# A Mamba-2 mixer's decays: repeated rows loaded from memory and subtracted on ScalarE, in place of a product on TensorE

## The reference

```
proj = hidden @ in_proj_w.T                    # gate, (x, B, C), dt
xBC  = silu(causal_conv4(proj[x, B, C]))       # 4 taps per channel
dt_p = softplus(dt + dt_bias);  A = -exp(A_log)
for t:  state = state * exp(dt_p*A)[t] + (dt_p*x)[t] * B[t]     # 64 heads, 64 x 128
        y[t]  = state @ C[t]
y    = y + x*D;  yn = group_rms(y) * norm_weight * silu(gate);  out = yn @ out_proj_w.T
```

## Time and profile before

| what | value |
|---|---|
| time, median of 3 runs | 1298.97 us |
| the profiled execution | 1300.67 us |
| its span in the trace | 1298.9 us |
| TensorE busy | 1230.5 us, 95% |
| VectorE busy | 933.9 us, 72% |
| ScalarE busy | 702.5 us, 54% |
| GpSimd busy | 653.6 us, 50% |
| moved by DMA | 57.52 MB, 44 GB/s |

### The profile page before, as it was taken

The page is one execution under the profiler, slowest core; times in us unless marked ns, Lnnn a source line. Parts: engine busy times, 40 slices in busy tenths (PEclk is TensorE's granted clock), DMA queues, the critical chain, the costliest instruction groups (busy, mean ns, idle before and its releaser), DMA issues. The chain is left out here.

```text
span 1298.9 us, 22009 instructions
## 1 busy us (share of the span) xinstructions
PE 1230.5 (95%) x6680; PEld 968.9 (75%) x6690; DVE 933.9 (72%) x1735; ACT 702.5 (54%) x1056; POOL 653.6 (50%) x707
## 2 busy tenths in 40 slices
PE   5999999999999999999999999999679999889976
PEld 4777777787778778777778878777557777667754
DVE  5786778669667866966886696688567555479995
ACT  3676676567567666756766675665543333222210
POOL 5057546655655655565465556545653343433330
PEclk9999999999999999999999999999789999889996
DMA  5111021011102101110210110010103322211100
GB/s 178 46 50 34 2 67 34 19 34 49 33 1 66 33 17 33 50 32 1 66 32 17 33 58 24 5 34 2 41 17 115 97 90 83 93 49 48 45 16 25
DMA packets 44233, 57.52 MB, mean 44 GB/s; under 512 B 10117, under 2 KB 21159, under 8 KB 43929
## 3 DMA queue, kind: packets, MB, share of 16 engines
q1 hardware_dynamic: 44185, 56.92, 14.3%
HBM read 49.95 MB, written 6.96 MB: 44 GB/s over the span
## 5 line engine op out<-in xcount | busy, mean ns | idle before, releaser
L722 DVE SCALAR_TENSOR_TENSOR conv<-p_tile,conv_taps,conv 128x511 f32<-128x511 f32 x189 | 141.3, 748 | 51.4 <-ACT conv L583 36.4
L831 DVE TENSOR_TENSOR em<-em,p_gb 128x512 f32<-128x512 f32 x128 | 82.1, 683 | 69.6 <-ACT em L630 69.5
L527 POOL TENSOR_TENSOR squares<-squares 128x256 f32<-128x256 f32 x64 | 48.0, 750 | 132.5 <-ACT squares L656 132.5
L94 PE MATMUL p_tile<-xn_hi,wc_hi 128*128 128x512 f32 x252 | 110.8, 440 | 0.9 <-DVE halo L726 0.9
L656 ACT ACTIVATE squares<-y 128x512 f32<-128x512 f32 x64 | 40.4, 631 | 112.5 <-DVE y L867 111.5
L722 DVE SCALAR_TENSOR_TENSOR conv<-p_gate,conv_taps,conv 128x511 f32<-128x511 f32 (+2 forms) x90 | 67.0, 745 | 46.7 <-ACT conv L583 43.1
L94 PE MATMUL p_tile<-xn_lo,wc_hi 128*128 128x512 f32 x252 | 98.8, 392 | 0.0
L94 PE MATMUL p_d<-wr_hi,zt_hi 128*128 128x512 f32 x236 | 94.0, 398 | 1.5 <-ACT em L630 1.5
L94 PE MATMUL p_d<-wr_lo,zt_hi 128*128 128x512 f32 x236 | 93.1, 394 | 0.0
L495 POOL TENSOR_TENSOR x_w<-xs,head_g 128x512 f32<-128x512 f32 x56 | 58.4, 1043 | 68.7 <-ACT xs L624 63.6
L588 ACT ACTIVATE xbc<-conv 128x512 f32<-128x512 f32 x96 | 60.7, 632 | 59.7 <-DVE conv L730 37.4
(11 more groups left out here) (393 smaller groups left out, 3605.1 us busy)
## 6 DMA issues: line engine op xcount, KB each, us to landing
w_raw<-w SPq DMA_DIRECT2D x108, 256.0 KB, 2.7
q_words<-q SPq DMA_DIRECT2D x33, 256.0 KB, 2.7
h_ring<-h_lo_rows SPq DMA_DIRECT2D x6, 704.0 KB, 4.8
h_lo_rows<-h_rest SPq DMA_DIRECT2D x11, 256.0 KB, 2.1
x_res<-x SPq DMA_DIRECT2D x8, 256.0 KB, 4.1
out<-out_t SPq DMA_DIRECT2D x8, 256.0 KB, 2.0
h_lo_rows<-h_rest SPq DMA_DIRECT2D x11, 128.0 KB, 1.9
gate_second<-w SPq DMA_DIRECT2D x4, 256.0 KB, 5.0
```

The lines of the kernel that those rows point to most:

```text
L94: pe.matmul(out, lhs(k)[0], rhs(k)[n], start=(start and k == 0 and n == 0), stop=False)
L722: ve.scalar_tensor_tensor(out=conv[:, s, sh:], in0=p[:, 0:HALF - sh], scalar=conv_w[:, bass.ds(g, 1), j, tap], in1=conv[:, s, sh:], op0=AL ...
L831: ve.tensor_tensor(m, m, gm.unsqueeze(1).broadcast_to([P, HG // 2, P]), ALU.mult)\
```

## The change

- TensorE's four spreading products (L1085) and two difference products (L1095) go, with their operands and the banks they wrote; `p_d0` and `p_d1` stay as banks of other products.
- cum itself (float32) is written to memory in the prologue, and so is exp(cum), which ScalarE makes there. For each chunk SyncE loads the row of the 8 heads (1024 numbers) into all 128 partitions of `em` (512 KB), and the exp(cum) rows into `e_cum` by two transfers of 64 partitions each, whose pieces are 512 bytes long.
- cum is transposed into a new table `cum_tok` (token on the partition). For the next chunk, ScalarE computes, in place and for each of the 8 heads, max(cum[s] - cum[t], 0) on 128 x 128 elements (`decay_steps`), right behind `z_round`; where the gate tile's SiLU stands behind `z_round`, it now stands behind these eight. In the chunk itself two exponentials with scale -1, in place, complete the decays. No large negative number is needed.
- ScalarE's exponential into `e_cum` goes (L628, L632).
- VectorE's splitting of cum (L961 to L967) goes, a copy into `cum_tok` comes. The transposes of the whole chunk's decay stand behind convolution tile 2 of the prologue, in bank `p_y`, and ScalarE's exponential of them waits there.
- Waits on the two difference banks go (for the output product, the sum of squares, p_in and row transposes); others take their place.

```diff
-        def load_d(g, c):
-            wait(sp, s_d, n - 1)
...
+        def load_cum(g, c):
+
+            n = g * NC + c
+            wait(sp, s_intra, n - 1)
+            row = at(sp, g + c * G)
+            sp.dma_start(em[:, c % 2, :], cum_rows.rearrange("c (g h) t -> (c g) (h t)", g=G)[bass.ds(row, 1), :]
+                         .broadcast_to([P, HG * P])).then_inc(s_dl[c % 2], 16)
+
+        def load_e_cum(g, c):
+
+            wait(sp, s_t, g * (NC - 1) + c - 1)
+            row = at(sp, g + c * G)
+            own = e_rows.rearrange("c (g j a) t -> (c g) a j t", g=G, a=2)[bass.ds(row, 1)]
+            for a in range(2):
+                sp.dma_start(by_tile(e_cum[a * HD:(a + 1) * HD, :]),
+                             own[:, a, :, :].broadcast_to([HD, GW // P, P])).then_inc(s_ecl, 16)
...
             for c in range(NC):
+                if c + 1 < NC:
+                    load_e_cum(g, c + 1)
                 if c + 2 < NC:
-                    load_d(g, c + 2)
+                    load_cum(g, c + 2)
...
+        def decay_steps(g, c):
+
+            act.wait_ge(s_dl[c % 2], 16 * (g * (NC // 2) + c // 2 + 1))
+            for h in range(HG):
+                steps = em[:, c % 2, h * P:(h + 1) * P]
+                made = act.activation(steps, steps, ACT.Relu, scale=-1.0, bias=cum_tok[:, c, bass.ds(g * HG + h, 1)])
+            made.then_inc(s_e, 1)
...
-                act.wait_ge(s_d, n + 1)
-                wait(act, s_intra, n - 1)
-                if last and c >= CH:
-                    act.activation(e_cum[:], p_in[:], ACT.Exp).then_inc(s_ec, 1)
-                for k, p in enumerate((p_d0, p_d1)):
-                    act.activation(em[:, c % 2, k * 512:(k + 1) * 512], p[:], ACT.Exp).then_inc(s_e, 1)
-                if c > 0 and not (last and c >= CH):
-                    act.activation(e_cum[:], p_in[:], ACT.Exp).then_inc(s_ec, 1)
+                act.wait_ge(s_e, 3 * n + 1)
+                for k in range(2):
+                    decay = em[:, c % 2, k * 512:(k + 1) * 512]
+                    act.activation(decay, decay, ACT.Exp, scale=-1.0).then_inc(s_e, 1)
...
                 z_round(n, y_bank(last, c))
+                if c < NC - 1:
+                    decay_steps(g, c + 1)
+                elif not last:
+                    decay_steps(g + 1, 0)
                 if made and c % CH >= 2:
                     gate_silu(CH + n, made[1], made[2], gate_bank(c))
...
+        act.wait_ge(dt_tp, 4)
+        act.activation(by_half(etot_t), transposed(p_y), ACT.Exp).then_inc(dt_ac, 1)
...
-                pe.wait_ge(s_dl[c % 2], 32 * (g * (NC // 2) + c // 2 + 1))
-                if c > 0:
-                    wait(pe, s_t, g * (NC - 1) + c - 1)
-                    for j in range(GW // P):
-                        pe.matmul(p_in[:, j * P:(j + 1) * P], head_rows[:, j, :], d_lhs[:, c % 2, :],
-                                  start=True, stop=True)
-                wait(pe, s_e, 2 * n)
...
-                for k, p in enumerate((p_d0, p_d1)):
-                    mm = pe.matmul(p[:], d_lhs[:, c % 2, :], d_rhs[:, c % 2, k * 512:(k + 1) * 512],
-                                   start=True, stop=True)
-                mm.then_inc(s_d, 1)
...
                 if c > 0:
 
                     pe.wait_ge(s_stu, g * (NC - 1) + c)
-                    pe.wait_ge(s_ec, g * (NC - 1) + c)
+                    wait(pe, s_t, g * (NC - 1) + c - 1)
...
             conv_tile(j, 0, j, 0, (p_tile, p_d1)[j % 2])
+            if j == 2:
+                pe.wait_ge(dt_ve, 12)
+                for b in range(CH):
+                    mm = pe.transpose(p_y[:, b * P:(b + 1) * P],
+                                      t_cum[:, (b + 1) * P - 1:(b + 1) * P].broadcast_to([P, P]), ident[:])
+                mm.then_inc(dt_tp, 1)
```

More of the change, by code:

```diff
@@ L172, in mixer @@
     gm = p_gb[:, 2 * P:3 * P]
-    parts = nc.dram_tensor("cum_parts", [G, PART, HG, L], BF16, kind="Internal").ap()
+    cum_rows, e_rows = (nc.dram_tensor(k, [NC, H, P], F32, kind="Internal").ap() for k in ("cum_rows", "e_cum_rows"))
     w_rows = io["w"].rearrange("n p c -> (n p) c")
@@ L192, in mixer @@
         sem(f"l2_{k}") for k in ("st", "var", "rs", "xn", "tr", "hi", "lo"))
[L194 to L198, removed]
+    s_xt, s_gb, s_prj, s_gate, s_ss, s_out, s_inter, s_intra, s_stn = (
+        sem(f"pe_{k}") for k in ("xt", "gb", "prj", "gate", "ss", "out", "inter", "intra", "stn"))
+    s_xs, s_e, s_cin, s_xc, s_sg, s_zhi, s_sq, s_whi = (
+        sem(f"act_{k}") for k in ("xs", "e", "cin", "xc", "sg", "zhi", "sq", "whi"))
     s_head = sem("ve_head")
@@ L339, in mixer @@
     t_w = y[:]
-    t_parts = [x[:, 0:GW // 2].bitcast(BF16) for x in (x_dt, x_w, x_d)]
+    t_ecum = x_d[:]
     t_mask = squares[:, 0:GW // 2].bitcast(BF16)
@@ L398, in sync @@
             load_w(0, w)
-        for k in range(PART):
-            wait(sp, dt_ve, 12 + k)
+        for rows, made in ((cum_rows, (ln_st, NC + 3)), (e_rows, (dt_ac, 6))):
+            sp.wait_ge(*made)
             for a in range(2):
[L403 to L408, removed]
+                heads_a = (t_cum if rows is cum_rows else t_ecum)[a * H:(a + 1) * H, :]
+                sp.dma_start(rows[a * CH:(a + 1) * CH].rearrange("c h t -> h c t"),
+                             heads_a.rearrange("h (c t) -> h c t", t=P)).then_inc(s_parts, 16)
+        sp.wait_ge(s_parts, 16 * 4)
+        load_cum(0, 0)
+        sp.wait_ge(dt_tp, 4)
+        sp.wait_ge(dt_ve, 11)
+        load_cum(0, 1)
         def group(g, last):
             for c in range(NC):
+                if c + 1 < NC:
+                    load_e_cum(g, c + 1)
                 if c + 2 < NC:
-                    load_d(g, c + 2)
+                    load_cum(g, c + 2)
                 elif not last:
-                    load_d(g + 1, c + 2 - NC)
+                    load_cum(g + 1, c + 2 - NC)
                 if not last:
@@ L697, in scalar @@
         gate_silu(3, 3, 0)
+        act.wait_ge(dt_ve, 13)
+        decay_steps(0, 0)
         group(0, False)
@@ L1038, in row_transpose @@
             if p_row[k] is p_d1:
-                pe.wait_ge(s_e, 2 * (n + 1))
+                wait(pe, l2_lo, {2: 1}.get(k, 0))
                 if k == NC - 2:
@@ L1080, in group @@
                 pe.matmul(p_gb[:, 0:P], xbc[:, TB, cs], xbc[:, TC, cs], start=True, stop=True).then_inc(s_gb, 1)
-                pe.wait_ge(s_dl[c % 2], 32 * (g * (NC // 2) + c // 2 + 1))
-                if c > 0:
-                    wait(pe, s_t, g * (NC - 1) + c - 1)
-                    for j in range(GW // P):
-                        pe.matmul(p_in[:, j * P:(j + 1) * P], head_rows[:, j, :], d_lhs[:, c % 2, :],
-                                  start=True, stop=True)
-                wait(pe, s_e, 2 * n)
-                wait(pe, s_res, n - 2 if tail and c > CH else n - 1)
-                wait(pe, s_v, n - 1)
                 if first:
                     pe.wait_ge(s_tap, TILES * TAPS)
-                for k in rows_in(last, c - 1):
-                    pe.wait_ge(l2_lo, k + 1)
-                for k, p in enumerate((p_d0, p_d1)):
-                    mm = pe.matmul(p[:], d_lhs[:, c % 2, :], d_rhs[:, c % 2, k * 512:(k + 1) * 512],
-                                   start=True, stop=True)
-                mm.then_inc(s_d, 1)
                 for tile in now:
```

76 lines of the change are left out of this document (18 added, 58 removed).

## The result

The changed kernel took **1343.1 us** (median of 4 runs, 1341.99 to 1344.66) against 1297.7 for the kernel before (4 runs beside it): 1.034 times as long, 95% interval 1.032 to 1.037. The forecast was 1335, in a range of 1280 to 1362. Its profiled execution took 1341.99 us, with a span of 1340.2: 41.3 us more span than before.

What follows compares the result with a forecast made beforehand. It took the loop through ScalarE and VectorE to overtake TensorE as the bound, 4.3 us a group slower: 1300.7 + 34 (groups) + 3 (prologue) = 1338, set against the median 1335 us, range 1280 to 1362.

Steps and rivals of the forecast that it cites:

- What bounds the kernel: Loop groups: TensorE's queue sets the 113.02 us; a closed ScalarE-VectorE loop beside it has 0.4 us slack in short chunks.
- ScalarE's part: Between z_round and xs: eight differences add 2.4 us a chunk, 0.30 each, with bounds of 0.9 and 5 us.
- Rivals 1 and 2: Price of the eight differences: under 1.4 us, TensorE stays bound, 1262 us (0.21); or 3.0 us, 1366 us (0.09).
- The loop's sum: One group, z_round to z_round: pieces sum to 116.0 us, 117.3 with c5's extra, against 113.0 before.
- TensorE's answer in c5: In c5 TensorE's tile 2 waits for c4's gate SiLU, adding 1.3 us to the loop.
- TensorE's relief: TensorE's queue: removed spreads and difference products save 0.67 us a chunk, 0.44 in c0, 5.1 us a group.
- rival 1: Whole kernel: TensorE stays the bound and gets faster, 1262 us; chance 0.21.
- c0 to c3 of the last group: Last group's first four chunks: 60.4 us against 56.5, so 4 us slower.
- Transfers: Loads of em, e_cum and the weights behind them stay hidden: 0 taken, between 0 and 20 us.
- Prologue: ScalarE waits for transposes behind TensorE's tile 2, conv 2 starts 3.4 us late; 3 us taken.
- Tail: Last group's c4 to c7: the stall only moves, banks come free sooner; 0, with 3 us either side.
- x_w stands as it is: Last group's c4: GpSimd's x_w is unchanged, so TensorE's 2.23 us idle stall only moves.

Runs made afterwards that it cites:

- experiment 4: Kernel before, all products kept, with eight extra 128 x 128 ScalarE operations with a per-partition bias behind each rounding of groups 0 to 6: 1419.7 us.
- experiment 7: Changed kernel with the eight differences ahead of ScalarE's wait for y and the loop over groups written out on ScalarE and VectorE: 1279.0 us.
- experiment 3: Changed kernel with the repeated rows' loads into em and e_cum made tiny behind the first two chunks: 1343.9 us.
- experiment 10: Changed kernel with ScalarE's prologue wait for the last transposes, and the exponential behind it, moved behind the last of its first SiLUs: 1338.4 us.
- experiment 2: Changed kernel with the eight differences moved from behind z_round to ahead of ScalarE's wait for y, loop kept: 1293.7 us.
- experiment 1: Changed kernel with two differences of 128 x 512 in place of the eight of 128 x 128: 1296.6 us.

## Why the prediction was right, point by point

- **What bounds the kernel** (TensorE, with a loop of 0.4 us slack beside it): the loop was there. Putting the differences into it made 113.0 into 118.0 us a group; the same differences outside it gave 112.3, or 109.7 with the loop written out. What it missed is the second loop, exponential to output product, which experiment 4 laid open. The change removes that tie, so the miss cost nothing here; that was luck, as the prediction had not looked at it.
- **ScalarE's part**: 2.4 us for eight, 0.30 each, by subtracting 384 columns from the 512-wide operation. Measured 2.35. Rivals 1 and 2 were two prices for this block, and both fall. A 512-wide difference costs 1.23 / 2 = 0.62, the price of the earlier trace rows.
- **The loop's sum**: within 0.1 us in seven chunks of eight, TensorE's answer in c5 included. c0 was 0.5 short behind a branch back, and right without one. It worked because each piece was the interval between two events of the same engine pair in a trace of the loop; those intervals held the register costs (c3, c6 and c7 shrink by 0.4 to 0.5 when written out) without my knowing of them.
- **TensorE's relief, 5.1 us a group**: the mis-sized term, 3.3 to 3.6 by experiment 7 (in its queue 0.48 a chunk in place of 0.67, 0.25 in c0: 7 x 0.48 + 0.25 = 3.6). I had counted the slow pick-up of the convolution's second product, 0.20 us, as part of the removed products; behind the transposes alone half of it stays (0.33 to the next product instead of 0.43). The forecast doesn't hang on it, as TensorE stopped being the bound, but rival 1's 1262 does: by 8 x 3.3 us less and the prologue's 3 more it becomes 1276.
- **c0 to c3 of the last group, 4 us**: wrong, 0.5. The prediction set its 60.4 us against 56.5, which is what TensorE takes for c0 to c3 of a loop group. In the last group these chunks took 58.3 us already before, 14.27 of them in c3, and 58.8 after, with 14.27 in c3 again. The seven groups ahead of it came to 31.7 where 30 were forecast.
- **Transfers, 0**: right (experiment 3).
- **Prologue, 3 us**: the wait was about right in size (experiment 10), but the first chunk's own eight differences, 2.3 us ahead of xs, were left out of the term: xs came 5.8 us late, the first rounding 5.4. TensorE waited 3.58 us for that chain, to 54.64, and its granted clock from 40 to 60 us was 0.91 where it had been 1.00; that too is in the 5.4.
- **Tail, 0 with 3 either side**: 3.4, of which c6 of the last group is 2.3 (12.66 to 15.01), c4 0.7 and c5 0.3. "x_w stands as it is" was wrong there: x_w is made from xs, and xs now stands behind the eight differences. TensorE's p_x waits for x_w in c4 (7.24 us), c5 and c6 (5.13 each), and most of that takes the place of waits that it had at other products. ScalarE, then TensorE, in c6:
```profile
981.00 2.43 ACT L599 ACTIVATE em<-em,cum_tok 128x128 f32<-128x128 f32 x8
983.33 0.58 ACT L631 ACTIVATE xs<-p_x 128x512 f32<-128x512 f32 x1
```
```profile
985.13 2.04 PE L1112 MATMUL p_x<-x_w,b_tok 128*128 128x512 f32 x2 [5.13 <-POOL x_w L494]
```
GpSimd, which makes x_w, had waited 2.40 us for that xs. From the transposes of x (978.12) to that product are 7.01 us, where they were 6.16 (939.53 to 945.69): 0.85 of c6's 2.3. The rest is the clock. TensorE in c6 before and after (length, busy, granted clock, DMA):
```profile
941.91:954.60 12.69, 9.85 (x57) 0.87 0.00 0
```
```profile
980.50:995.50 15.00, 10.31 (x51) 0.77 0.39 101
```
The output product and what follows it, to the second layer's transposes, took 4.75 us (987.25 to 992.00) at a granted clock of 0.56, and 3.39 (947.68 to 951.07) at 0.83 before: 1.4 us for the same work.
- **Not in the sum at all**: the branch back, 0.5 us a group by the table.

The sum, 1337.7 us for the profiled execution, came out 4.3 short of its 1342.0: 2.4 in the prologue, 1.7 in groups 0 to 6 (the branches' 0.5 for each of five are in them), 3.4 in the tail and 0.4 behind it, less the 3.6 too many for c0 to c3 of the last group. So a part of the closeness of the number is luck: a wrong comparison made good what the prologue and the tail lacked. The mechanism and the price of the eight are not touched by that. The other 4 us of the 8 between 1335 and the median are the step from profiled execution to median (1.7 one way before, 1.1 the other way after) and a rounding.

## What to carry to other kernels

A busy share of 95% doesn't say that freeing that engine pays: look for the chains beside it that come back to their start within a few tenths of a microsecond of its period, and price what you add by whether it stands inside them. The same eight operations, moved from behind the rounding to ahead of the wait for y, took 49 us off the changed kernel, and 50 where the loop is written out (1329.0 to 1279.0). A wait that shows up once in a trace can be a tie with no slack: add a known delay to find out. Once the covering engine is relieved, look at the first operation behind each branch back of a loop.

## What the runs showed that was not expected

- A branch back can hold VectorE for 2.4 to 5.9 us with no releaser in the profile, and brings 5 packets on the instruction queue. Thirty idle instructions ahead of the loop brought it about in a kernel that did not have it.
- How much of it is felt seems to depend on how much work an engine still has queued: in the changed kernel ScalarE had eight operations left to run behind its last wait ahead of the branch and lost 0.3 to 0.5 us; in experiment 2, with those moved forward, it lost 3.2 to 3.8. That the depth is the reason is an inference from the two timelines.
- Written out, groups of VectorE's taps lose pauses of 0.2 us each that stand in the looped form.
- Waits of TensorE are followed by stretches at a lower granted clock: 0.85 in c0 of experiment 1 behind a wait of 2.5 us, 0.77 in the last group's c6 behind 5.13, where the kernel before has 1.00 throughout its loop and 0.87 in that c6. Not every such wait did it: in experiment 2 four c0 of five stayed at 1.00.
